# The gated second bias of a mixture of experts: from tiled fp32 products to two full products on a block diagonal

## The reference

```
logits = einsum('btd,de->bte', x, Wr) + br
gates = softmax(where(selected two, logits, -inf))      # 8 gates per token, six of them zero
h = relu(einsum('btd,edh->bteh', x, W1) + b1)
out = einsum('bte,bteh,ehd->btd', gates, h, W2)
out = out + einsum('bte,ed->btd', gates, b2)            # the gated second bias
```

## Time and profile before

| | us |
|---|---|
| median of 3 runs | 209.75 (209.21 to 209.9) |
| span of the profiled execution | 207.8 |
| PE busy | 199.5 (96%) |
| PE weight loads busy | 176.5 (85%) |
| DVE busy | 167.8 (81%) |
| ACT busy | 132.2 (64%) |
| POOL busy | 112.3 (54%) |

### The profile page before, as it was taken

The page is one execution under the profiler, slowest core; times in us unless marked ns, Lnnn a source line. Parts: engine busy times, 40 slices in busy tenths (PEclk is TensorE's granted clock), DMA queues, the critical chain, the costliest instruction groups (busy, mean ns, idle before and its releaser), DMA issues.

```text
span 207.8 us, 4986 instructions
## 1 busy us (share of the span) xinstructions
PE 199.5 (96%) x1752; PEld 176.5 (85%) x1752; DVE 167.8 (81%) x453; ACT 132.2 (64%) x316; POOL 112.3 (54%) x132
## 2 busy tenths in 40 slices
PE   6999988798999999999999999999999999999995
PEld 6845976686799979997999799998998899789994
DVE  6398769889789999899788988898999888556633
ACT  2236748697568847797677767677757776345441
POOL 8502647869976378629561966376746674010000
PEclk9999999999999999999999999999999999999999
DMA  6649595716515133423140504241000000000000
GB/s 175 160 127 286 153 279 148 224 46 183 158 62 145 69 108 106 103 76 104 41 147 25 170 3 151 57 144 36 0 0 28 0 2 3 25 3 2 25 3 25
DMA packets 20264, 18.70 MB, mean 90 GB/s; under 512 B 1776, under 2 KB 18704, under 8 KB 20240
## 3 DMA queue, kind: packets, MB, share of 16 engines
q1 hardware_dynamic: 17344, 16.85, 28.0%
q10 hardware_dynamic: 2896, 1.54, 2.8%
HBM read 11.83 MB, written 6.55 MB: 88 GB/s over the span
## 4 chain that ended last, share of the span: by engine, by line
PE 91%; DVE 3%; ACT 2%; issue 1%; POOL 1%; POOLq 0%; ACTq 0%; DVEq 0%
PE y_ps L436 28%; PE h_ps L421 22%; PE score_ps L361 7%; PE misc_ps L380 6%; PE score_ps L349 6%; PE h_ps L369 4%; PE score_ps L277 3%; PE misc_ps L401 2%; PE score_ps L338 2%; PE score_ps L421 2%; PE misc_ps L389 2%; PE misc_ps L287 1%; PE misc_ps L327 1%; PE misc_ps L306 1%; PE misc_ps L300 1%
## 5 line engine op out<-in xcount | busy, mean ns | idle before, releaser
L695 ACT ACTIVATE hT<-h_ps,b_sb 128x256 f32<-128x256 f32 x118 | 49.4, 470 | 33.3 <-PE h_ps L421 32.1
L436 PE MATMUL y_ps<-w_sb,hT 128*128 128x128 f32 x508 | 68.0, 277 | 0.0
L436 PEld LDWEIGHTS y_ps<-w_sb,hT 128*128 128x128 f32 x508 | 62.8, 191 | 3.5 <-issue 2.2
L1188 POOL TENSOR_TENSOR half_sum<-e_sb 128x512 f32<-128x512 f32 x28 | 37.3, 1332 | 30.8 <-ACT e_sb L667 30.5
L938 DVE TENSOR_TENSOR attn<-e_sb,e_rcp 128x1024 f32<-128x1024 f32 x32 | 42.1, 1319 | 3.3 <-ACT e_rcp L678 3.3
L930 DVE TENSOR_REDUCE shift_m<-score_ps 128x128 fp32r<-128x1024 f32 x32 | 38.7, 1212 | 2.2 <-PE score_ps L338 1.1
L421 PE MATMUL h_ps<-x1T_hi,w_lo 128*128 128x256 f32 x118 | 37.7, 320 | 1.5 <-ACT hT L695 0.9
L667 ACT ACTIVATE e_sb<-score_ps 128x1024 f32<-128x1024 f32 x32 | 32.8, 1024 | 5.6 <-PE score_ps L361 5.4
L1007 DVE SCALAR_TENSOR_TENSOR acc<-y_ps,gates,acc 128x128 f32<-128x128 f32 x96 | 29.0, 342 | 8.6 <-PE y_ps L436 7.3
L421 PE MATMUL h_ps<-x1T_hi,w_hi 128*128 128x256 f32 x118 | 33.1, 280 | 0.0
L421 PE MATMUL h_ps<-x1T_lo,w_hi 128*128 128x256 f32 x118 | 33.1, 280 | 0.0
(11 more groups left out here) (117 smaller groups left out, 291.3 us busy)
## 6 DMA issues: line engine op xcount, KB each, us to landing
k_scratch<-k_parts SPq DMA_DIRECT2D x14, 256.0 KB, 2.6
k_stack<-k_scratch SPq DMA_DIRECT2D x14, 256.0 KB, 4.0
q_stack<-q_scratch SPq DMA_DIRECT2D x28, 128.0 KB, 2.7
q_scratch<-q_parts SPq DMA_DIRECT2D x7, 256.0 KB, 2.7
w_sb<-in_w SPq DMA_DIRECT2D x1, 1024.0 KB, 6.6
out_y<-y_out SPq DMA_DIRECT2D x7, 128.0 KB, 1.9
x_all<-in_x ACTq DMA_DIRECT2D x1, 768.0 KB, 6.2
ctxT<-in_ctx_t SPq DMA_DIRECT2D x1, 640.0 KB, 6.1
```

The source lines that it names most:

```text
L436: mm = nc.tensor.matmul(product(j, t), hT[:, j % 2, c, t * P:(t + 1) * P], w2_sb[:, e * HC + c, :], start=(c == 0), stop=(c == HC - 1))
L695: op = nc.scalar.activation(hT[:, j % 2, c, :], hidden(j)[:, c * S:(c + 1) * S], ACT.Relu, bias=b1_sb[:, e * HC + c:e * HC + c + 1])
L1188: nc.gpsimd.tensor_tensor(half_sum[:], e[:, 0:HQ // 2], e[:, HQ // 2:HQ], ALU.add).then_inc(sum_step, 1)
```

## The change

The product with b2 becomes two full products (one for each half of the tokens) with 128 rows and 128 columns of the array, in fp32r, which PE does in a single pass. To keep the precision, gates and b2 are split in a high and a low fp32r part. `gate_parts` holds for each token 32 columns: high, low, high, low gates. `b2_rows` holds on the 32 rows of a group b2's high part twice and its low part twice. Since a full product sums over all 128 partitions, the gates must lie on a block diagonal: `block_gates` on POOL multiplies the transposed gates with a mask of the groups (`group_of`) into `gatesD`.

New work: on DVE `split_b2` once, with two reductions, one copy and one multiply-add; on DVE a copy and a subtraction in front of each transpose; on POOL `block_gates` once a batch. PE waits for `gates_blocked` where it waited for `gatesT_made`. b2 is loaded by one DMA to all partitions instead of four small ones.

```diff
             def gated_b2(b, freed, n):
                 if b == 0:
-                    pe.wait_ge(small_in, 112)
+                    pe.wait_ge(b2_rows_made, 1)
                 wait(pe, freed, n)
-                pe.wait_ge(gatesT_made, b + 1)
+                pe.wait_ge(gates_blocked, b + 1)
                 for t in range(TT):
-                    for g in range(P // 32):
-                        rows = slice(32 * g, 32 * g + E)
-                        mm = nc.tensor.matmul(misc_ps[32 * g:32 * g + 32, t * P:(t + 1) * P], gatesT[rows, t, :],
-                                              b2_sb[rows, :], start=True, stop=True)
+                    mm = nc.tensor.matmul(misc_ps[:, t * P:(t + 1) * P], gatesD[:, t, :, :].rearrange("p g k -> p (g k)"),
+                                          b2_rows[:], start=True, stop=True)
                 mm.then_inc(b2_done, 1)
...
-            for g in range(P // 32):
-                act.dma_start(b2_sb[32 * g:32 * g + E, :], b2).then_inc(small_in, 16)
+            act.dma_start(b2_sb[:], b2.unsqueeze(0).to_broadcast([P // E, E, D])).then_inc(small_in, 16)
...
+            def split_b2(b):
+                dve.wait_ge(neg_ident_made, 1)
+                nc.vector.tensor_reduce(neg_lo_row[:], neg_ident[:].bitcast(F32).rearrange("p (g r) -> p g r", r=32)[:, :, 16:24],
+                                        AX.XY, ALU.min)
+                nc.vector.tensor_reduce(group_of[:], ident[:].rearrange("p (g r) -> p g r", r=32), AX.X,
+                                        ALU.max).then_inc(b2_step, 1)
+                dve.wait_ge(small_in, 64)
+                nc.vector.tensor_copy(b2_hi[:], b2_sb[:]).then_inc(b2_step, 1)
+                dve.wait_ge(b2_step, 2)
+                nc.vector.scalar_tensor_tensor(out=b2_rows[:], in0=b2_hi[:].bitcast(F32), scalar=neg_lo_row[:, 0:1], in1=b2_sb[:],
+                                               op0=ALU.mult, op1=ALU.add).then_inc(b2_rows_made, 1)
 
             def transpose_gates(b):
                 dve.wait_ge(gates_made, b + 1)
-                wait(dve, b2_done, b)
+                if b == 0:
+                    dve.wait_ge(gates_zeroed, 1)
+                nc.vector.tensor_copy(gate_parts[:].rearrange("p t (k s) -> p t k s", s=2 * E)[:, :, :, 0:E],
+                                      gates[:, b % 2].unsqueeze(2).to_broadcast([P, TT, 2, E])).then_inc(gate_step, 1)
+                dve.wait_ge(gate_step, 2 * b + 1)
+                nc.vector.tensor_tensor(gate_parts[:, :, E:2 * E], gates[:, b % 2], gate_parts[:, :, 0:E].bitcast(F32),
+                                        ALU.subtract).then_inc(gate_step, 1)
+                dve.wait_ge(gate_step, 2 * b + 2)
+                wait(dve, gates_blocked, b)
                 nc.vector.transpose(gatesT[:].rearrange("p t e -> p (t e)"),
-                                    gates[:, b % 2].rearrange("p t e -> p (t e)")).then_inc(gatesT_made, 1)
+                                    gate_parts[:].bitcast(F32).rearrange("p t e -> p (t e)")).then_inc(gatesT_made, 1)
...
                 choose_experts(0)
                 normalize(1, 1)
+                split_b2(0)
                 k_lo(3)
                 head_max(2, 1)
                 make_gates(0)
...
+            def block_gates(b):
+                if b == 0:
+                    pool.wait_ge(b2_step, 1)
+                pool.wait_ge(gatesT_made, b + 1)
+                wait(pool, b2_done, b)
+                nc.gpsimd.tensor_tensor(gatesD[:], gatesT[:].unsqueeze(2).to_broadcast([P, TT, P // 32, 32]),
+                                        group_of[:].unsqueeze(1).unsqueeze(3).to_broadcast([P, TT, P // 32, 32]),
+                                        ALU.mult).then_inc(gates_blocked, 1)
...
                 if there(now):
                     head_sum(now, 0)
                     head_sum(now, 1)
+                if there(g):
+                    block_gates(g)
                 if there(f):
                     ln2_end(f)
...
                 head_sum(2, 1)
+                block_gates(0)
                 ln2_end(1)
                 split_w1(7)
...
                 head_sum(3, 1)
+                block_gates(1)
                 ln2_end(2)
```

More of the change, by code:

```diff
@@ L57, in build @@
         b2_sb = sb("b2_sb", [P, D])
+        b2_hi = sb("b2_hi", [P, D], F32R)
+        b2_rows = sb("b2_rows", [P, D], F32R)
+        neg_lo_row = sb("neg_lo_row", [P, 1])
+        group_of = sb("group_of", [P, P // 32])
         wr_sb = sb("wr_sb", [P, E])
@@ L112, in build @@
         gated_onehot = sb("gated_onehot", [P, 2, TT, E])
-        gates = sb("gates", [P, 2, TT, 32])
+        gates = sb("gates", [P, 2, TT, E])
+        gate_parts = sb("gate_parts", [P, TT, 32], F32R)
         gatesT = sb("gatesT", [P, TT, 32])
+        gatesD = sb("gatesD", [P, TT, P // 32, 32], F32R)
         hT = sb("hT", [P, 2, HC, S])
@@ L131, in build @@
             sem("ident_zeroed"), sem("ident_made"), sem("pool_made"), sem("neg_ident_made"), sem("neg_half_made"))
+        b2_step, b2_rows_made = sem("b2_step"), sem("b2_rows_made")
         v_zeroed, q_zeroed = sem("v_zeroed"), [sem("q_zeroed0"), sem("q_zeroed1")]
@@ L155, in build @@
             sem("gates_made"))
-        gates_zeroed, gatesT_made, b2_done, b2_added = (
-            sem("gates_zeroed"), sem("gatesT_made"), sem("b2_done"), sem("b2_added"))
+        gates_zeroed, gate_step, gatesT_made, gates_blocked, b2_done, b2_added = (
+            sem("gates_zeroed"), sem("gate_step"), sem("gatesT_made"), sem("gates_blocked"), sem("b2_done"), sem("b2_added"))
         h_done, relu_made, y_done, gated = sem("h_done"), sem("relu_made"), sem("y_done"), sem("gated")
@@ L690, in relu @@
                 if j == 0:
-                    act.wait_ge(small_in, 112)
+                    act.wait_ge(small_in, 64)
                 act.wait_ge(h_done, j + 1)
@@ L922, in split_wr @@
             def split_wr():
-                dve.wait_ge(small_in, 112)
+                dve.wait_ge(small_in, 64)
                 nc.vector.tensor_copy(wr_pair[:, 0, :], wr_sb[:]).then_inc(wr_hi_made, 1)
@@ L953, in choose_experts @@
                     dve.wait_ge(pool_made, 1)
-                    dve.wait_ge(gates_zeroed, 1)
                 at = ROUTER_STEPS * b
@@ L981, in make_gates @@
                 dve.wait_ge(router_step, at + 4)
-                nc.vector.tensor_tensor(gates[:, b % 2, :, 0:E], gated_onehot[:, 0], gated_onehot[:, 1],
+                nc.vector.tensor_tensor(gates[:, b % 2], gated_onehot[:, 0], gated_onehot[:, 1],
                                         ALU.add).then_inc(gates_made, 1)
+            def split_b2(b):
[4 more added lines that the diff above has]
+                                        ALU.max).then_inc(b2_step, 1)
+                dve.wait_ge(small_in, 64)
+                nc.vector.tensor_copy(b2_hi[:], b2_sb[:]).then_inc(b2_step, 1)
+                dve.wait_ge(b2_step, 2)
+                nc.vector.scalar_tensor_tensor(out=b2_rows[:], in0=b2_hi[:].bitcast(F32), scalar=neg_lo_row[:, 0:1], in1=b2_sb[:],
+                                               op0=ALU.mult, op1=ALU.add).then_inc(b2_rows_made, 1)
             def transpose_gates(b):
                 dve.wait_ge(gates_made, b + 1)
-                wait(dve, b2_done, b)
+                if b == 0:
[7 more added lines that the diff above has]
+                wait(dve, gates_blocked, b)
                 nc.vector.transpose(gatesT[:].rearrange("p t e -> p (t e)"),
-                                    gates[:, b % 2].rearrange("p t e -> p (t e)")).then_inc(gatesT_made, 1)
+                                    gate_parts[:].bitcast(F32).rearrange("p t e -> p (t e)")).then_inc(gatesT_made, 1)
             def add_expert(b, e):
@@ L1209, in period @@
             def period(i):
-                now, f = i - 2, i - 3
+                now, f, g = i - 2, i - 3, i - 4
                 if there(now):
@@ L1256, in _ @@
                                     pattern=[[-1, P]], channel_multiplier=1).then_inc(ident_made, 1)
-            nc.gpsimd.memset(gates[:], 0.0).then_inc(gates_zeroed, 1)
+            nc.gpsimd.memset(gate_parts[:].bitcast(F32), 0.0).then_inc(gates_zeroed, 1)
             pool.wait_ge(neg_half_made, 2)
```

## The result

The changed kernel takes 215.7 us (median of 4 runs, 214.51 to 216.47) where the one before takes 209.75 us. The ratio is 1.0285 with a 95% interval of 1.0249 to 1.0322, so it is slower by 2.5% to 3.2%. The profiled execution took 216.21 us with a span of 214.4 us, 6.6 us above the 207.8 of the earlier trace rows.

The account below looks back on a forecast made before the run. PE, 91% of the chain, was taken to bound the kernel. To 209.75 us it added -3.85 (PE's block), +4.1 (batch 0), +1.7 (batch 1) and +2.7 (batches 2 to 4), giving 214.4 us, range 209.9 to 215.8.

Parts of the forecast that it names:

- PE's block: b2 products on PE: cheaper products and following group save 0.55 us a batch, 3.85 us over batches 1 to 7.
- POOL's block of batch 0: PE's first b2 product waits for block_gates behind head_sum(2, 1) on POOL, starting at 58.5 us: +4.1 us.
- The price of DVE's lateness: split_b2 on DVE delays subtract_max(2, 1) on PE by 1.2 to 1.8 us, hidden inside batch 0's wait.
- the sum, +4.1: Batch 0's net loss on PE: 4.4 us late less 0.35 us for the shorter block, range 2.3 to 5.8.
- Batch 1: Gate copy on DVE waits for POOL's half_sum(3, 1); PE loses 1.7 us at project_k(5), 0.4 without a collision.
- Batches 2 to 4: Gate subtraction on DVE starts 0.03 us behind half_sum and waits; PE loses 0.9 us each, +2.7 us together.
- The first rival: In batches 2 to 4 DVE gets in before POOL, so no collision: 211.7 us, chance 0.25.
- The dear product: New b2 product no cheaper than full-size fp32, 0.44 us a block, 1.8 us more: 216.2 us, chance 0.06.
- Faster: PE's saving decides: batch 0's block ready before 57.4 us, DVE loses no lock: 208.6 us, chance 0.12.
- Small edits at nothing: One DMA instead of four and a smaller zeroed tile, first 7 us: no effect, 0.1 us either way.

Follow-up runs that it names:

- experiment 5: Kernel before, with the eight tiled fp32 products per batch replaced by two full fp32r products on w1_hi operands, no new DVE or POOL work: 206.15 us, ratio 0.9842.
- experiment 6: Changed kernel without the subtraction that makes the low part of the gates, in all batches: 211.69 us, ratio 1.0092.
- experiment 7: Changed kernel with transpose_gates(g) moved behind normalize(f, 3) on DVE, in the regular periods alone: 212.58 us, ratio 1.0148.
- experiment 1: Changed kernel with split_b2 moved earlier on DVE, between head_max(1, 0) and normalize(0, 3): 217.04 us, ratio 1.0366.
- experiment 2: Changed kernel with block_gates(0) moved on POOL ahead of head_sum(2, 0): 213.69 us, ratio 1.0202.
- experiment 3: Changed kernel with both split_b2 behind head_max(1, 0) on DVE and block_gates(0) ahead of head_sum(2, 0) on POOL: 211.12 us, ratio 1.0065.
- experiment 4: Changed kernel with eight small unused fp32 products on PE between expert_up(0, 4) and attend_values(1): 215.04 us, ratio 1.0267.
- experiment 8: Changed kernel with split_b2 and block_gates(0) earlier, transpose_gates(1) behind add_residual(2), and transpose_gates in regular periods behind normalize(f, 3): 207.59 us, ratio 0.9894.

## Why the prediction was right, and where not

The forecast was 214.4 us, 2.2% slower; measured 215.7, 2.85% slower, in the range of 209.9 to 215.8. Most of its steps held:

- **PE's block.** 0.55 us saved where it stands, as forecast, shown alone by experiment 5. The parts of it were off: the products cost 0.17 us together, not 0.22, and the group behind keeps 0.05 of the 0.20 us. What reaches the end is 0.5 us a batch and 0.2 in batch 0.
- **POOL's block of batch 0.** Forecast ready at 58.5 us; it was ready at 58.50. That it fits to the hundredth is luck: the sums in front ended 0.85 us later than before, not the 0.6 that I took from the middle of a wide range, and the block took 0.61 us, not 0.74, with no gap in front. And the step from there to PE was wrong in the profile. I had PE through expert_down(0, 2) before 58.5 and waiting for about 3 us. In fact the attn pair and q_lo(3) on DVE held PE until 55.16, and PE came to the product at 59.29, after it was ready. At full clock it does wait, but 0.47 us (experiments 6 and 7). The price of DVE's lateness was seen for subtract_max(2, 1) (forecast 1.2 to 1.8, measured 1.4 us), and the attn pair behind was put down as falling inside the wait. The gate copy meeting half_sum(2, 0) in batch 0, 1.0 us, was not in the working at all, nor was the addition of the gates that meets w_lo, 0.5 us. That the sum, +4.1, was met (4.5 us between 46 and 57 us) is luck in the profile, for it came by this other route: 1.4 + 1.9 us for waiting on DVE, 1.4 us for the clock, less 0.2. The chain through POOL and the one through DVE happen to end within 1 us of each other; experiments 1 to 3 separate them.
- **The clock.** Missing in the forecast. Wherever I let PE wait for microseconds I priced the wait alone. It lengthened attend_values(1) by 1.4 us in the profile, and by their mean clock that is so in two of the four runs. Not all of it reaches the end: at full clock PE waits 0.47 us for POOL instead, and batch 0 costs 3.9 us, not 4.5 (experiment 7). That the two pairs of runs differ by 1.5 us is more than this 0.6, and the rest is open.
- **Batch 1.** Forecast +1.7, measured +1.5 (5.2 to 6.7): the copy took 1.22 us; the subtraction got in 0.01 us ahead of quarter_sum, so it was the cheap one of the two cases. PE lost it earlier than forecast: 1.3 us at expert_down(1, 2), which waits for add_expert(1, 0), and only 0.1 us at project_k(5), the step that I had named.

```profile
79.62 1.22 DVE L1004 CAST gate_parts<-gates 128x32 fp32r<-128x32 f32 x1
...
79.52 1.28 POOL L1212 TENSOR_TENSOR half_sum<-e_sb 128x512 f32<-128x512 f32 x1
```

- **Batches 2 to 4.** Forecast 0.9 us each, at 0.03 us behind half_sum; measured 1.0 us each, at 0.03 us. This was the step on which most hung, taken as a little better than even. Experiments 6 and 7 show the meeting as the cause. The first rival (no collision, 211.7) falls. Experiment 7 is that case nearly by itself, at 212.6 us.
- **The dear product** (0.44 us a block) falls with 0.17. **Faster** falls: the block was not ready before 57.4, and DVE lost the exclusion in batches 0 to 4.
- **Small edits at nothing.** Not quite on DVE: its first operation took 1.88 us where it took 3.69. Experiments 3 and 4 show 1.88 as well, but the other five with the same edit show 3.63, so the edit does not settle it. In the first 7 us PE's difference to before stays within 0.3 us.

**The first 46 us** differ between any two profiles here. At 46 us PE stood between 1.1 us ahead of the profile of before (experiment 1) and 1.3 us behind it (experiment 4). Only rows such as this one of experiment 8 show why, a weight load that lands later:

```profile
43.39 1.16 PE L441 MATMUL y_ps<-w_sb,hT 128*128 128x128 f32 x8 [0.76 <-DMA w_sb<-in_w]
```

So a single span cannot tell a microsecond here, and the readings above take the growth of the difference at a place, not its value. What sets the landing of the loads was not tried.

## What to carry to other kernels

Before moving work from a full engine to idle ones, write down beside which instructions of the other engine the new ones will start: an operation of 0.17 us can cost 1.3 if it shares a port with a long one, and a helper step placed behind two long sums is as late as they are. Where a step is not needed at once, put it where its wait is not on anyone's path; here the same work in other places turned a loss of 2.85% into a gain of 1.1%. And a wait of the matrix engine is to be priced with the clock it may cost afterwards.

## What the runs showed of the hardware that I had not expected

- VectorE and GpSimd exclude each other even at a lead of 0.03 us, and the same in three periods: half_sum at 98.43, the subtraction at 98.46, duration 1.28 in place of 0.17 us. At the same offset a transpose is not held (0.25 us at +0.02 us, experiment 6), nor is a reduction (group_of, 0.27 us, started at 45.20 behind half_sum at 45.17). I had known rows with a lead of 0.08 us only the earlier trace rows. The order of the starts decided in each case that I read. This is the rule of the Trainium skill, page "SBUF — State Buffer", section "SBUF: two separate sides", that whoever starts first keeps the port pair, and the rows agree with it down to that lead.
- TensorE's granted clock fell to 0.50 (1.2 GHz) in an idle time of 3.9 us (experiment 1) and stayed so for more than 5 us of work behind it, in all four runs by their mean clock; behind 1.9 us (the changed kernel) its mean over 3.2 us was 0.57, in two of four runs, and in experiment 7 it was 1.00 behind the same 1.88 us. With the idle time filled it stayed at 1.00 in all four runs.
